# End of the mixer layer: the x products of the next step issued before the output products, one semaphore per input, squares added on GpSimd, and the later phases' weights issued in pieces from SyncE

## The reference, cut to what matters

```
zxbcdt = x @ W_in
z  = zxbcdt[..., :512]
xs = zxbcdt[..., 512:1024]
...
y = SSD_SCALE * ys + D_param * xh          # xh is xs by heads
g = y * silu(z)
y = g * rsqrt(mean(g * g) + EPS) * norm_w
x = layernorm(x + y @ W_out)
```

## Time and profile before

| | us |
|---|---|
| median of 3 runs | 2977.25 (2970.6 to 2991.64) |
| profiled execution, its own time | 2990.1 |
| span of the profiled execution | 2988.2 |
| first instruction of `finish_mixer` (SP, POOL, ACT) | 1666.0 |
| first matmul of the phase | 1705.2 |
| first instruction of the next phase | 1987.05 |

### The profile page before, as it was taken

How to read it: one execution, slowest core, us unless ns; L and a number is a source line. 1 busy time by engine, 2 the same in 40 slices (tenths; PEclk the granted TensorE clock), 3 DMA queues, 4 the chain that set the end, 5 groups by cost and what they waited for, 6 DMA issues and landing times. The chain is left out here.

```text
span 2988.2 us, 63411 instructions
## 1 busy us (share of the span) xinstructions
PE 2247.6 (75%) x19953; PEld 1651.9 (55%) x19954; DVE 1957.2 (65%) x5279; ACT 1539.1 (52%) x3098; POOL 1452.5 (49%) x2255
## 2 busy tenths in 40 slices
PE   7882777877777777877777288878488857767887
PEld 4551555555555555554555277766344435546887
DVE  3443898988889889888889223336432227765676
ACT  3445888888888787878886011125311112222222
POOL 2224777777777777777677100014311124433444
PEclk8875898898999988888898689888799988888898
DMA  4656666666666665656665723234322223331111
GB/s 120 180 159 159 149 164 152 161 156 162 152 161 157 160 157 148 158 147 156 159 153 138 217 89 102 88 99 141 110 69 68 70 73 101 112 95 49 45 42 36
DMA packets 303154, 374.46 MB, mean 125 GB/s; under 512 B 54116, under 2 KB 242854, under 8 KB 302438
## 3 DMA queue, kind: packets, MB, share of 16 engines
q1 hardware_dynamic: 286358, 331.96, 42.4%
q0 software_dynamic: 9872, 27.28, 2.7%
q10 hardware_dynamic: 6688, 12.23, 1.3%
HBM read 151.03 MB, written 86.05 MB: 79 GB/s over the span
## 5 line engine op out<-in xcount | busy, mean ns | idle before, releaser
L690 PE MATMUL p_ps_sc<-p_CR,p_BR 64*128 64x128 f32 x4096 | 342.8, 313 | 181.8 <-DVE p_M L946 159.9
L609 POOL TENSOR_TENSOR p_CR<-p_pc 128x256 f32<-128x256 f32 x512 | 373.2, 729 | 128.4 <-DVE p_pc L933 101.9
L690 PEld LDWEIGHTS p_ps_sc<-p_CR,p_BR 64*128 64x128 f32 x4096 | 291.3, 213 | 241.6 <-issue 216.7
L823 ACT ACTIVATE p_D<-p_ps_x 128x512 f32<-128x512 f32 x512 | 289.4, 592 | 236.9 <-PE p_ps_x L656 236.5
L613 POOL TENSOR_TENSOR p_BR<-p_pb 128x256 f32<-128x256 f32 x512 | 373.1, 729 | 25.5
L933 DVE SCALAR_TENSOR_TENSOR p_pc<-p_ps_c,p_beta,p_cs 128x256 f32<-128x256 f32 x512 | 243.7, 476 | 150.8 <-DMA p_sn<-p_tr_s 132.9
L946 DVE TENSOR_TENSOR p_M<-p_ps_sc,p_D 128x512 f32<-128x512 f32 x512 | 328.2, 682 | 11.6 <-PE p_ps_sc L690 10.6
L600 POOL TENSOR_TENSOR p_tr_s<-p_xt,p_mg 128x256 f32<-128x256 f32 x256 | 186.5, 729 | 224.8 <-DMA p_sn<-p_tr_s 195.4
L705 PE MATMUL p_ps_y<-p_M,p_uexp 128*32 128x128 f32 x4096 | 291.5, 296 | 2.9 <-ACT p_D L823 2.5
L705 PEld LDWEIGHTS p_ps_y<-p_M,p_uexp 128*32 128x32 f32 x4096 | 230.2, 119 | 44.2 <-issue 31.9
L933 DVE SCALAR_TENSOR_TENSOR p_pc<-p_ps_c,p_beta,p_sn 128x256 f32<-128x256 f32 x512 | 243.3, 475 | 0.0
(11 more groups left out here) (276 smaller groups left out, 5442.3 us busy)
## 6 DMA issues: line engine op xcount, KB each, us to landing
p_cs<-p_tr_c SPq DMA_DIRECT2D x512, 128.0 KB, 2.4
p_sn<-p_tr_s SPq DMA_DIRECT2D x512, 128.0 KB, 2.4
p_phib<-scratch_phi SPq DMA_DIRECT2D x256, 128.0 KB, 3.1
p_x<-scratch_rt SPq DMA_DIRECT2D x72, 128.0 KB, 2.0
scratch_ro<-p_o POOLq DMA_DIRECT2D x72, 128.0 KB, 2.0
p_xT<-in_xT SPq DMA_DIRECT2D x64, 128.0 KB, 3.1
scratch_u<-p_u SPq DMA_DIRECT2D x16, 512.0 KB, 3.8
scratch_wu<-p_wu SPq DMA_DIRECT2D x16, 512.0 KB, 5.0
```

Of the source, the lines that this page charges most:

```text
L609: e.tensor_tensor(CR[:, p, g, :], pc[:, g % 2, 0, :], pc[:, g % 2, 1, :], ALU.add).then_inc(S["rotC"], 1)
L690: m = e.matmul(sc_ps[half][:, (g * 2 + b) * L:(g * 2 + b + 1) * L], BR[half * 64:half * 64 + 64, p, 2 * q + g, b * L:(b + 1) * L], CR[half ...
L823: e.activation(D[:, n, :], x_ps[i % 2][:, :], ACT.Exp).then_inc(S["x_ok"], 1)
```

## The change

TensorE's step is written in another order. `of_x(t + 1)` (the x products of the next step) now stands between the z products of step t and its output products; the output products wait for `g_ok` (g itself) and no longer for the squares; `o_mm` is set right behind them; the transposes of step t - 1 come behind them, and last the sums of squares, over one tile `total` of 256 columns, 2 products in place of 8. GpSimd makes `total` with two additions (`halves`, then `total`) from the four blocks of squares. VectorE forms `mix` of step t + 1 right behind g of step t (`mixed`), and ScalarE makes the squares ahead of the copy of the transposes. y, xT and x have a semaphore pair each. `load_ahead` is a generator with 43 DMAs (the large ones cut: `w13` in 9, `w2` in 3, the three int8 matrices in 2 each), and SyncE takes three of them at the end of each of its steps, in its own program, behind the load of x. ScalarE issues none. SyncE's steps are all written out.

```
 def load_ahead(e, I, W):
     e.dma_start(K["w1"][:, :, :], I["sw1"].rearrange("(k p) n -> p k n", p=P)).then_inc(got, 16)
+    yield
...
-    e.dma_start(K["w13"][:, :, :, :], I["w13"].rearrange("(k p) e n -> p k e n", p=P)).then_inc(got, 16)
-    e.dma_start(K["w2"][:, :, :, :], I["w2"].rearrange("(k p) e n -> p k e n", p=HIDE // 2)).then_inc(got, 16)
+    for n in range(NE + 1):
+        e.dma_start(K["w13"][:, :, n, :], I["w13"].rearrange("(k p) e n -> p k e n", p=P)[:, :, n, :]).then_inc(got, 16)
+        yield
+    for n in range(0, NE + 1, 3):
+        e.dma_start(K["w2"][:, :, n:n + 3, :], I["w2"].rearrange("(k p) e n -> p k e n", p=HIDE // 2)[:, :, n:n + 3, :]).then_inc(got, 16)
+        yield
...
         @block.sync
-            def load(t, p):
+            def load_y(t, p):
+                at_least(e, S["mix_ok"], t, 2, -2)
+                e.dma_start(y[:, p, :, :], W["y"].rearrange("(k c) r t -> c r k t", k=NB)[t, :, :, :]).then_inc(S["y_in"][p], 16)
+            def load_xT(t, p):
                 at_least(e, S["z_mm"], t, 1, -1)
...
+            def load_x(t, p):
                 at_least(e, S["xr_ok"], t, 2, -2)
...
-            stream(e, load, store)
+            ahead = load_ahead(e, I, W)
+            for t in range(2):
+                load_xT(t, t)
+                load_y(t, t)
+                load_x(t, t)
+            for t in range(NC):
+                if t + 2 < NC:
+                    load_y(t + 2, t % 2)
+                    load_xT(t + 2, t % 2)
+                if t:
+                    store(t - 1, (t - 1) % 2)
+                if t + 2 < NC:
+                    load_x(t + 2, t % 2)
+                for _ in range(3):
+                    next(ahead, None)
+            store(NC - 1, 1)
...
         @block.gpsimd
             def step(t, p):
+                at_least(e, S["g2_ok"], t, 2, 2)
+                e.tensor_tensor(halves[:, :, :], g2[:, 0:2, :], g2[:, 2:4, :], ALU.add).then_inc(S["half_ok"], 1)
+                at_least(e, S["half_ok"], t, 1, 1)
+                at_least(e, S["q_mm"], t, 1, 0)
+                e.tensor_tensor(total[:, :], halves[:, 0, :], halves[:, 1, :], ALU.add).then_inc(S["sum_ok"], 1)
...
         @block.tensor
-            def step(t, p):
-                at_least(e, S["x_in"][p], t - p, 32, 64)
+            def of_x(t, p):
+                at_least(e, S["xT_in"][p], t - p, 16, 32)
                 at_least(e, S["mix_ok"], t, 2, 0)
...
-                if not (isinstance(t, int) and t == 0):
-                    turn(t - 1, 1 - p)
-                at_least(e, S["g2_ok"], t, 2, 2)
+                if not (isinstance(t, int) and t == NC - 1):
+                    of_x(t + 1, 1 - p)
+                at_least(e, S["g_ok"], t, 2, 2)
                 at_least(e, S["xr_ok"], t, 2, 0)
                 for b in range(BATCH):
                     for n in range(NB):
                         m = e.matmul(o_ps[:, b * DM:(b + 1) * DM], g[:, n, b * L:(b + 1) * L], w_out[:, n, :],
-                for b in range(BATCH):
-                    for n in range(NB):
-                        m = e.matmul(q_ps[:, b:b + 1], g2[:, n, b * L:(b + 1) * L], ones[:, :], start=(n == 0), stop=(n == NB - 1))
                 m.then_inc(S["o_mm"], 1)
-            two_step_loop(e, step, NC)
+                if not (isinstance(t, int) and t == 0):
+                    turn(t - 1, 1 - p)
+                at_least(e, S["sum_ok"], t, 1, 1)
+                at_least(e, S["ms_ok"], t, 1, 0)
+                for b in range(BATCH):
+                    m = e.matmul(q_ps[:, b:b + 1], total[:, b * L:(b + 1) * L], ones[:, :], start=True, stop=True)
+                m.then_inc(S["q_mm"], 1)
+            of_x(0, 0)
+            two_step_loop(e, step, NC, 2, 2)
...
         @block.scalar
-            load_ahead(e, I, W)
-
...
         @block.vector
-            def step(t, p):
-                at_least(e, S["x_in"][p], t - p, 32, 64)
+            def mixed(t, p):
+                at_least(e, S["y_in"][p], t - p, 8, 16)
...
+                if not (isinstance(t, int) and t == NC - 1):
+                    mixed(t + 1, 1 - p)
-                at_least(e, S["o_mm"], t, 1, 1)
+                at_least(e, S["q_mm"], t, 1, 1)
```

More of the change, by code:

```diff
@@ L1149, in finish_mixer @@
         g2 = sb("g2", [P, NB, CT])
+        halves, total = sb("halves", [P, 2, CT]), sb("total", [P, CT])
         ms, rms = sb("ms", [P, BATCH]), sb("rms", [P, BATCH])
@@ L1222, in step @@
                 m.then_inc(S["xs_mm"], 1)
+            def step(t, p):
                 at_least(e, S["silu_ok"], t, 2, 0)
@@ L1258, in step @@
                     e.activation(sz[:, 2 * n:2 * n + 2, :].rearrange("p n t -> p (n t)"), z_ps[n][:, :], ACT.Silu).then_inc(S["silu_ok"], 1)
-                if not (isinstance(t, int) and t == 0):
-                    copy_turned(t - 1, 1 - p)
-                at_least(e, S["o_mm"], t, 1, 0)
+                at_least(e, S["sum_ok"], t, 1, 0)
                 for n in range(2):
@@ L1264, in step @@
                     e.activation(g2[:, 2 * n:2 * n + 2, :], g[:, 2 * n:2 * n + 2, :], ACT.Square).then_inc(S["g2_ok"], 1)
+                if not (isinstance(t, int) and t == 0):
+                    copy_turned(t - 1, 1 - p)
             two_step_loop(e, step, NC)
@@ L1303, in step @@
                 norm_vector(e, S, N, t, xr, x1[:, p, :, :], free)
-            two_step_loop(e, step, NC)
+            mixed(0, 0)
+            two_step_loop(e, step, NC, 2, 2)
 def stream(e, load, store):
@@ L1714, in _ @@
             e.wait_ge(S["tab_in"], 16)
-            e.wait_ge(W["k6_in"], 48)
+            e.wait_ge(W["k6_in"], 16 * 13)
             def expert(j):
@@ L2223, in _ @@
         def _(e):
-            e.wait_ge(const_in, 16 * 8)
+            e.wait_ge(const_in, 16 * 11)
             e.wait_ge(S["const_in"], 16 * 2)
```

51 lines of the change are left out of this document (36 added, 15 removed).

## The result

The changed kernel took 2873.73 us (median of 4 runs, 2859.13 to 6434.76) against 2984.44 (median of 4, 2970.6 to 2996.77), a ratio of 0.962 [0.958, 0.966]: 3.8% faster. One of its runs took 6434.76 us, for a cause that the record doesn't show: the ratio leaves it out, the median of 4 doesn't, and the other three (2859.13, 2861.11 and 2886.35) have a median of 2861.11. Six more runs of the same kernel beside other experiments had a median of 2861.98 and a ratio of 0.9619 [0.9588, 0.965]. The prediction was 2861.

A forecast was written before the change was run, and what follows sets the result against it. The prediction took one chain (z, silu, g, squares, output) to bound the phase, with its pauses and slow clock. Savings of 27.4 + 5.2 + 77.0 + 6.3 = 115.9 us turned the median 2977.25 into 2861, range 2848 to 2888.

The forecast's parts named there:

- start of TensorE: Phase head: without y stuck in the DMAs, TensorE starts at 1677.7 in place of 1705.13, 27.4 us less.
- start to the first Q: From TensorE's start to the end of the first sums of squares: 16.2 us in place of 21.4, 5.2 less.
- The step: Length of a usual step if TensorE waits for nothing: 3.46 + 3.35 + 3.35 + 0.60 + 0.50 = 11.26 us.
- Full clock: Output products in each step: assumed at 2.4 GHz, taking 3.35 us, since denser work has less reason to lose the clock.
- g ready at Q + 6.16: Each step: g done 6.16 us after the previous sums of squares end, half a microsecond before the output products need it.
- The squares by way of GpSimd: Each step: GpSimd's two additions give `total` at 9.3 us, needed at 10.6; hidden with 1.3 us to spare.
- The weights on SyncE: Three weight DMAs per step: at about 300 GB/s the fullest step needs 11.1 us; xT hidden by a microsecond.
- Rival 2: Weight steps: DMAs full at 224 GB/s in five steps, 13 us more, giving 2874; chance 0.11.
- Rival 1: Every step: the clock is not held and 1.65 us of half clock stay, 25 us back, giving 2886; chance 0.05.
- Rival 3: Every step: a VectorE or GpSimd chain overruns its margins by 1.8 us, 27 us back, giving 2888; chance 0.06.
- Rival 4: 13 steps: weight pieces hold SyncE 17 us each, TensorE waits for xT, 133 us back, giving 2994; chance 0.03.
- Rival 5: Phase head: TensorE starts as late as some other input, so 27.4 us come back, giving 2888; chance 0.02.

The follow-up runs named there:

- experiment 1: The kernel before with only the later phases' weights moved to SyncE, three pieces behind each step's store: ratio 0.9903, phase 288.12 us.
- experiment 4: The changed kernel with each step's x products and mix back at the head of their own step: ratio 0.9727, phase 242.31 us.
- (3): The changed kernel with the sums of squares as 16 one-column matmuls on TensorE and no GpSimd additions: ratio 0.9678, phase 226.24 us.
- (5): The changed kernel with x products at the head of their own step and 16 one-column matmuls for the squares: 2940.24 us in one run, phase 280.56.
- experiment 7: The changed kernel with six weight DMAs per step, or all 43 in step 0, in place of three per step: 2877.27 and 2898.13 us, one run each.
- experiment 6: The changed kernel with the output products waiting for the squares in place of g: 2889.54 us in one run, phase 212.61.

## Why the prediction was right

Its sum was 115.9 us for the phase and 113.7 were measured. Term by term:

| term | predicted | measured |
|---|---|---|
| start of TensorE | 27.4 | 27.1 (39.1 to 12.0) |
| start to the first Q | 5.2 | 4.1 (21.4 to 17.4) |
| steps 1 to 14 | 77.0 | 76.5 (158.1 in place of 234.6) |
| step 15 | 6.3 | 6.3 (10.63) |
| tail | 0 | -0.2 |

*The start* came out within 0.3 us, and experiment 1 gets the same start with this part alone. Inside it two errors met: the constants take 9.4 us from the phase's first load to the first fold where 8.3 were reckoned, and TensorE starts 0.2 us behind the second fold where some 0.7 were reckoned. *Start to the first Q* was mis-sized by 1.1 us. I had put the first x products at the 5.36 of the row before, and they took 6.28, nearly all at half clock; in other profiles they took 4.74 to 5.75. The tenths for the activation table were not needed, since ScalarE had long loaded it.

*The step* was worked out as 11.26 and is 11.24 to 11.25 in the usual ones. *Full clock* was the assumption with the most on it, 25 us, and it held in steps 1 to 14. My reason, that a denser step has less cause to lose it, fits all profiles: no output products that followed the x products without a pause were slow. But the cause was named too simply. The text called the slow clock a consequence of the chain that makes the pause. With the pause and 4 one-column matmuls the clock fell in 1 step of 15 (experiment 4), with the 16 alone in none (3), with both in 11 of 15 (5). So in the steady steps either part would have brought most of the clock's gain by itself. That the pause alone never takes the clock isn't so: in the last step it did in five of eight profiles, 1.5 to 1.7 us each time, a term that the prediction didn't have and that the profiled run happened to be spared. *g ready at Q + 6.16*, half a microsecond early, is so in every second step; in the others 0.24 is left, in one 0.05, so the wait was avoided more narrowly than foretold. *The squares by way of GpSimd* are hidden with 1.67 to spare in the step shown and 1.1 at the least, predicted 1.3, with 1.27 and 0.73 for the additions, predicted 1.4 and 0.7.

*The weights on SyncE* were called hidden by a microsecond in the fullest step. There the DMAs are full at 1.01 with 274 GB/s (I had reckoned with 300), and TensorE waits 0.4 us for xT, which costs the step 0.65. The margin was nil and not one microsecond; what saved the sum is that it was one step, or two. Rival 2, with 224 GB/s in five steps, was off in its rate. Its mechanism is real, as the 7.7 and 35.6 us of experiment 7 show.

Rival 1 (25 us) didn't happen, and experiment 4 shows that a pause would seldom have been enough for it. Rival 3 is near: 0.67 us more in the chain already waits in nearly each step (experiment 6). Rival 4, with SyncE held in every step at 133 us in all, didn't happen: no single issue of SyncE in steps 1 to 14 of the profiled run, nor a group of two or three, took over 2 us, and all the weights queued at once cost 35.6 us. Rival 5 is excluded by the start at 12.0.

One reading in the prediction mixes two kinds of rows: in its list of a step's pieces the pause of 2.34 and the 5.41 are those of the matmuls, the others of the weight loads, and the list adds up to 17.00, not 16.88. By the weight loads alone the pause is 2.58 and the output products take 5.03. The forecast uses neither.

The measured median lies 12.7 above the forecast in one set of runs, all but 0.1 of it by the run of 6434.76 (2861.11 without it), and 1.0 above it in another of the same kernel. Runs of this kernel spread over 27 us (2855.27 to 2881.85 in six), and the median of the kernel before moved from 2977.25 to 2984.44 with one run more, so the hit to one microsecond is luck; the table above is what was right.

## What to carry to other kernels

Before an engine's pause is filled with other work, write down what is late next and by how much: here 0.05 to 0.50 us on g in most steps and 1.1 or more on `total` decided between 113 us and less, and both could be worked out to some tenths from the trace before. One step is not enough for such a margin: read it in several. Loads for later phases belong on a queue in which nothing stands behind them that is needed soon, in pieces no larger than a step can hide; on a compute engine's queue they delay that engine's first instruction by all their issues. And where two things together bring a cost (here the pause and the 16 one-column matmuls, and the clock), an edit that removes one of them can take away nearly all of it, so the two shouldn't both be credited with it.

## What the runs showed of the hardware

- TensorE's clock. An idle time of 2.50 us before the output products of each step left them at 3.32 us in 14 of 15 steps, at a granted clock of 1.00 over 30 us, when 4 one-column matmuls stood in each step. With 16 of them, the same 2.50 us idle and the same 25.80 us busy in 30, the output products took 5.01 in 11 of 15 steps, with the granted clock at 0.50 (1.2 GHz) for a part of them and 0.94 over 30 us. In the last step, 2.98 us idle with 4 of them left 3.32 in three profiles, and 3.64 us (one profile) or 2.98 us (four) gave 4.84 to 5.01. What in the 16 matmuls makes the difference is open: their number, their single column, or their place. This wasn't tried apart.
- The first products of the phase took 4.74 to 6.28 us in different profiles for the same 16 passes, 3.32 at full clock. They change level on the way: in the profiled run the granted clock is 0.50 from 1664 to 1670 and 1.00 from 1671.
- GpSimd's additions of f32 take 1.27 us for 512 columns and 0.73 for 256, beside the 1.384 and 0.729 of the earlier trace rows. VectorE's mix took 1.28 beside such an addition, and 1.28 in the head without one.
- A DMA share of 1.01 to 1.07 went with anything from 274 to 367 GB/s, by what was moved: a full share says nothing of the rate.
